# A shifted-window attention block and a ConvNeXt-V2 block in one launch: how the parameters and constants reach the chip

## What is computed

```
# block 0: window attention (7x7 windows, shifted by 3, 3 heads of 16), then an MLP
xw  = windows(roll(layernorm_over_channels(x) * norm1_g + norm1_b, -3, -3))      # 49 tokens each
q, k, v = split(xw @ qkv_w + qkv_b)
a   = softmax(q @ k.T * 16 ** -0.5 + bias)        # bias[h,i,j] = rel_bias_table[rel(i,j), h]
x   = x + roll(unwindow((a @ v) @ proj_w + proj_b), 3, 3)
x   = x + gelu(layernorm(x) @ fc1_w + fc1_b) @ fc2_w + fc2_b                     # 48 -> 192 -> 48
# block 1: depthwise 7x7 convolution, MLP with global response normalisation
y   = layernorm(dwconv7x7(x, dw_w) + dw_b) * ln_g + ln_b
y   = gelu(y @ w1.T + b1)
n   = sqrt(sum_over_pixels(y ** 2)); n = n / (mean_over_channels(n) + 1e-6)
x   = x + (grn_g * (y * n) + grn_b + y) @ w2.T + b2
```

## Time and profile before

| | us |
|---|---|
| median of 3 runs | 2145.37 |
| lowest and highest of the 3 | 2136.65, 2146.94 |
| profiled execution, whole | 2144.79 |
| profiled execution, span of the trace | 2142.8 |
| PE busy | 1776.0 (83%) |
| ACT busy | 1558.6 (73%) |
| DVE busy | 1510.8 (71%) |
| POOL busy | 1174.1 (55%) |
| hardware DMA queue, share of 16 engines | 43.0% |

### The profile page before, as it was taken

The page is one execution under the profiler, slowest core; times in us unless marked ns, Lnnn a source line. Parts: engine busy times, 40 slices in busy tenths (PEclk is TensorE's granted clock), DMA queues, the critical chain, the costliest instruction groups (busy, mean ns, idle before and its releaser), DMA issues. The chain is left out here.

```text
span 2142.8 us, 91033 instructions
## 1 busy us (share of the span) xinstructions
PE 1776.0 (83%) x38074; PEld 1038.0 (48%) x38074; DVE 1510.8 (71%) x2025; ACT 1558.6 (73%) x2884; POOL 1174.1 (55%) x1061
## 2 busy tenths in 40 slices
PE   1469889898989889898989898884799959888884
PEld 0245555555555555555555555551466622222221
DVE  1557878777787778777777878643677757767772
ACT  1458888888888888888888888873566648767770
POOL 1357777767677767777676777652255520111111
PEclk9979999999999999999999999995799967989998
DMA  2334343434434343434344353422378759988983
GB/s 21 76 92 114 88 117 85 114 96 103 103 96 110 89 119 84 115 90 108 98 102 104 96 114 87 100 50 63 85 217 217 214 121 189 225 213 209 229 206 106
DMA packets 241103, 260.66 MB, mean 122 GB/s; under 512 B 174431, under 2 KB 188148, under 8 KB 240713
## 3 DMA queue, kind: packets, MB, share of 16 engines
q1 hardware_dynamic: 225353, 215.94, 43.0%
q0 software_dynamic: 15360, 39.08, 6.3%
HBM read 159.26 MB, written 80.99 MB: 112 GB/s over the span
## 5 line engine op out<-in xcount | busy, mean ns | idle before, releaser
L439 POOL TENSOR_TENSOR shift<-const_b,qmax 113x588 bf16<-113x588 bf16 x256 | 344.6, 1347 | 53.9 <-DVE qmax L532 53.7
L464 POOL TENSOR_TENSOR xl<-x 113x784 bf16<-113x784 f32 x64 | 136.9, 2140 | 266.5 <-DVE x L554 266.5
L518 DVE TENSOR_TENSOR xh<-X,RS 113x784 f32<-113x784 f32 x64 | 228.7, 3573 | 19.2 <-DMA RS<-rs_scratch 18.4
L1505 POOL DMA_DIRECT2D out_rolled<-r_OUT x128 | 64.0, 503 | 322.3 <-DVE r_OUT L1607 319.3
L532 DVE TENSOR_REDUCE qmax<-ps_s 113x12 f32<-113x588 f32 x256 | 194.6, 760 | 61.4 <-PE ps_s L905 61.3
L758 ACT ACTIVATE G<-ps_m 128x392 f32<-128x392 f32 x384 | 184.1, 498 | 50.7 <-PE ps_m L1005 49.8
L726 ACT ACTIVATE P<-ps_t 113x588 f32<-113x588 f32 x256 | 171.9, 672 | 66.3 <-PE ps_t L955 65.5
L1340 PE MATMUL conv_ps<-xin,band_now 64*64 64x448 bf16 x2688 | 202.3, 364 | 4.1 <-DVE x_low L1242 4.1
L429 POOL TENSOR_TENSOR xhl<-xh 113x784 bf16<-113x784 f32 x64 | 203.4, 3178 | 2.5 <-DVE xh L572 2.5
L719 ACT COPY Uf<-ps_m 113x392 f32<-113x392 f32 x384 | 172.7, 485 | 32.1 <-PE ps_m L872 24.0
L524 DVE TENSOR_TENSOR Ul<-Uf 113x784 bf16<-113x784 f32 x192 | 180.6, 966 | 0.3 <-ACT Uf L719 0.2
(11 more groups left out here) (256 smaller groups left out, 5258.6 us busy)
## 6 DMA issues: line engine op xcount, KB each, us to landing
xin<-rows_scratch SPq DMA_DIRECT2D x96, 236.0 KB, 3.7
XT<-x_tokens SPq DMA_DIRECT2D x64, 294.0 KB, 4.7
X<-x_windows SPq DMA_DIRECT2D x128, 147.0 KB, 3.0
RS<-rs_scratch SPq DMA_DIRECT2D x128, 147.0 KB, 3.4
XR<-x_windows SPq DMA_DIRECT2D x128, 147.0 KB, 3.8
x_scratch<-x SPq DMA_DIRECT2D x128, 147.0 KB, 3.9
y_scratch<-y POOLq DMA_DIRECT2D x96, 196.0 KB, 2.8
r_RS<-rs_scratch SPq DMA_DIRECT2D x128, 147.0 KB, 3.9
```

The costliest lines, as they stand in the source:

```text
L439: nc.gpsimd.tensor_tensor(shift[:, j % 2], e, m, ALU.mult).then_inc(S["md"], 1)
L464: nc.gpsimd.tensor_tensor(xl1[:], x1[:, r, :], x1m[0][:, r, :], ALU.subtract).then_inc(S["x1_lo"], 1)
L518: nc.vector.tensor_tensor(xh0[:, r, :], X[:, r, :], RS[:, r, :], ALU.mult).then_inc(S["xh0"], 1)
```

## The change

All parameters and constants arrive in three arrays that the host lays out: `pack_a` (128 x 2039 f32) for the attention phase, `pack_c` (128 x 2176) for the convolution, `pack_r` (128 x 1160) for the last phase. Each is one tile, and the old names are views of it. The host also gathers the relative bias and casts the band constants.

```diff
-        center = sb("center", [R, R])
-        sums_f = sb("sums_f", [R, 2, R])
+        pack = sb("pack", [128, WIDE_A])
+        def packed(name, rows):
+            return pack[0:rows, PACK_A[name]]
+        center = packed("center", R)
+        sums_f = packed("sums", R).rearrange("p (a c) -> p a c", a=2)
...
-        CLEARS = 17
+        CLEARS = 5
-        SETUP_V = 41
-        BIAS_V = SETUP_V + 3
+        CLEAN_V, AUG_V, QK_V, GRAM_V, WV_V, SETUP_V = 5, 11, 13, 21, 25, 33
...
         def _(sp):
-            for tab, first, sign in ((tables[0], (REL - 1) * HEADS, -1), (tables[1], 0, 1)):
-                sp.dma_start(tab, bass.AP(tensor=prm["rel_bias_table"].tensor, offset=first,
-                                          ap=[[1, HEADS], [sign * HEADS, REL], [1, 1]]),
-                             allow_slow_non_contiguous=True).then_inc(table_turned, 16)
...
-            def later_loads():
-                sp.wait_ge(later["cleared"], len(later["zeros"]))
-                for dst, src in later["loads"]:
-                    sp.dma_start(dst, src).then_inc(later["loaded"], 16)
-                for row in edges:
+            def later_load(k):
+                dst, src = later["loads"][k]
+                sp.dma_start(dst, src).then_inc(later["loaded"], 16)
+            def margin_rows(k):
+                for row in edges[4 * k:4 * k + 4]:
                     sp.dma_start(rows_dram[:, row], margin[:].rearrange("c (b w) -> c b w", w=PAD)
                                  ).then_inc(margins_stored, 16)
...
-            sp.wait_ge(x_cleared, 6)
-            for raw in range(2):
-                tokens_load(Strip(0, raw, N))
-            setup_loads()
-            for raw in range(2 - TLEAD, -1):
-                step(Strip(0, raw, N), 0)
-            late_loads()
-            step(Strip(0, -1, N), 0)
-            later_loads()
-            for raw in range(N + 3):
+            tokens_load(Strip(0, 0, N))
+            sp.dma_start(pack[:], pack_a).then_inc(loaded, 16)
+            tokens_load(Strip(0, 1, N))
+            step(Strip(0, 2 - TLEAD, N), 0)
+            sp.wait_ge(x_cleared, 6)
+            for raw in range(3 - TLEAD, N + 3):
                 step(Strip(0, raw, N), (raw - 3) // STRIPS)
+                if raw in (STRIPS, STRIPS + 1):
+                    later_load(raw - STRIPS)
+                elif raw in (STRIPS + 2, STRIPS + 3):
+                    if raw == STRIPS + 2:
+                        sp.wait_ge(cleared, CLEARS)
+                    margin_rows(raw - STRIPS - 2)
...
         def _(pool):
-            for t in (proj_w, proj_b, fc2_b, w2_own, w2_part, bias_f, wv, wv_swap, *gram, *w1_own, *w1_part, margin, blank, x2):
+            for t in (wv, wv_swap, blank, margin, x2):
                 nc.gpsimd.memset(t[:], 0.0).then_inc(cleared, 1)
...
-            for raw in range(-4, -2):
+            for raw in range(-4, -1):
                 step(Strip(0, raw, N))
-            for t in later["zeros"]:
-                nc.gpsimd.memset(t, 0.0).then_inc(later["cleared"], 1)
-            steps(step, -2, N + 3)
+            for r in range(2):
+                pool.wait_ge(values_spread, 4 * r + 4)
+                nc.gpsimd.tensor_tensor(Ul[:, r, HEADS:, :], Uf[:, r, HEADS:, :], U[0][:, r, HEADS:, :], ALU.subtract
+                                        ).then_inc(values_low, 1)
+            steps(step, -1, N + 3)
...
 +            clear_inputs((X, RS), 0)
+            for t in (ps_t, ps_s, *ps_m):
+                link(nc.vector.memset(t[:], 0.0))
+            step(Strip(0, -4, N))
+            clear_inputs((XR,), 0)
+            clear_inputs((X, RS, XR), 1)
+            dve.wait_ge(loaded, 16)
...
 -                nc.scalar.preload_act_table_set("gelu_and_others")
+                if old.real:
+                    nc.scalar.preload_act_table_set("gelu_and_others")
...
-                nc.scalar.preload_act_table_set("natural_log_exp_and_others")
+                if old.real:
+                    nc.scalar.preload_act_table_set("natural_log_exp_and_others")
...
-            steps(step, -3, N + 2)
+            for raw in range(-3, -1):
+                step(Strip(0, raw, N))
+            act.wait_ge(setup_v, WV_V)
+            for r in range(2):
+                for a in range(2):
+                    for n, t in enumerate((wv, wv_swap)):
+                        nc.scalar.copy(
+                            Uf[:, r, HEADS + a, cols_of(n)].rearrange("p (w t) -> p w t", t=TOK),
+                            t[:, TOK * a:TOK * a + TOK].unsqueeze(1).to_broadcast([R, WINS // 2, TOK])
+                        ).then_inc(values_spread, 1)
+            steps(step, -1, N + 2)
...
 -            pe.wait_ge(setup_v, 6)
+            pe.wait_ge(setup_v, AUG_V)
...
-            pe.wait_ge(setup_v, SETUP_V)
+            pe.wait_ge(setup_v, GRAM_V)
...
+                    if s.n == 0 and j == 0:
+                        wait(pe, values_low, 2)
```

More of the change, by code:

```diff
@@ L244, in attention_phase @@
         x2_strips = x2_dram.rearrange("b c (g s i w) -> b s g c i w", g=2, s=STRIPS, i=WS)
[L247 to L270, removed]
-        blocks = []
-        for side in range(2):
-            for h in range(HEADS):
-                src = bass.AP(tensor=table_runs[side].tensor, offset=h * TOK * RUN,
-                              ap=[[RUN, TOK], [SPAN, WS], [1, WS]])
-                dst = bias_f[0:TOK, side, TOK * h:TOK * h + TOK]
-                blocks.append((dst.rearrange("p (a b) -> p a b", a=WS), src))
         block = ctx.enter_context(nc.Block())
@@ L608, in step, with clear_inputs @@
                 query_max(nxt, 1)
-            for t in (X, RS, XR):
-                for r in range(2):
+            def clear_inputs(tiles, r):
+                for t in tiles:
                     nc.vector.memset(t[:, r, :], 1.0).then_inc(x_cleared, 1)
-            for raw in range(-4, -2):
-                step(Strip(0, raw, N))
-            dve.wait_ge(cleared, CLEARS)
-            dve.wait_ge(loaded, 16 * len(loads))
+            clear_inputs((X, RS), 0)
+            for t in (ps_t, ps_s, *ps_m):
+                link(nc.vector.memset(t[:], 0.0))
+            assert chain[0] == CLEAN_V
+            step(Strip(0, -4, N))
+            clear_inputs((XR,), 0)
+            clear_inputs((X, RS, XR), 1)
+            dve.wait_ge(loaded, 16)
             link(nc.vector.tensor_copy(sum_w[:], sums_f[:]))
@@ L621, in _ @@
                 link(nc.vector.tensor_copy(aug[:, a, C:C + 1], norms[:, 2 * a + 1:2 * a + 2]))
+            assert chain[0] == AUG_V
+            step(Strip(0, -3, N))
             dve.wait_ge(setup_t, 1)
@@ L632, in _ @@
             link(nc.vector.tensor_tensor(out_b[:], proj_b[:], fc2_b[:], ALU.add))
-            splits = []
+            for g in range(2):
+                lo = ROWB * g
+                split(gram, lambda t: t[lo:lo + C + 1, :, lo:lo + C + 1],
+                      ps_s[lo:lo + C + 1, 0, 0:HEADS * (C + 1)].rearrange("p (h c) -> p h c", h=HEADS))
+            assert chain[0] == GRAM_V
+            dve.wait_ge(cleared, CLEARS)
             for g in range(2):
@@ L1826, in program @@
+def program(nc, x_in, x_tokens, packs, out_dram, images):
     scratch = {}
@@ L1837, in sb @@
             return ctx.enter_context(nc.sbuf_tensor(name, shape, dt))
-        tiles, zeros, loads = response_weights(nc, sb, layer1, con)
-        later = {name: ctx.enter_context(nc.semaphore("later_" + name)) for name in ("cleared", "loaded")}
+        tiles, loads = response_weights(nc, sb, packs[2])
+        later = {name: ctx.enter_context(nc.semaphore("later_" + name)) for name in ("loaded",)}
         with ExitStack() as inner:
@@ L1872 @@
     x_in, x_tokens = give("x_windows", windows), give("x_tokens", tokens_first(windows))
[L1873 to L1877 removed]
+    layers = [{k[8:]: np.asarray(a) for k, a in inputs.items() if k.startswith(f"L{n}_conv_")} for n in range(2)]
+    packs = [give("parameters_" + name, a) for name, a in zip("acr", packs_of(*layers, constants()))]
     out = nc.dram_tensor("out_rolled", (images, C, PLANE), F32, kind="ExternalOutput").ap()
[L1879 removed]
+    program(nc, x_in, x_tokens, packs, out, images)
     result = run_bass_kernel_spmd(nc, [arrays], core_ids=[0]).results[0]["out_rolled"]
```

247 lines of the change are left out of this document (127 added, 120 removed).

## The result

| | before | changed |
|---|---|---|
| median, us | 2143.34 (4 runs beside it) | 2075.66 (4 runs) |
| lowest and highest | 2136.65, 2146.94 | 2074.42, 2077.34 |
| ratio, 95% interval | | 0.9688 [0.9662, 0.9715] |
| profiled execution, and its span | 2144.79, 2142.8 | 2077.34, 2075.7 |

The changed kernel is 67.7 us faster by the medians and 67.1 by the spans; 2079 was forecast. Five more runs of it on another occasion gave 2073.53.

What follows compares the result with a forecast made beforehand. The attention pipeline's fixed beat was taken as unchanged, its start held back by setup and a stall. Setup 46.1 plus stall 19.6 gave 65.7 us off 2144.79, so 2079; range 2068 to 2096.

Steps and rivals of the forecast that it cites:

- Setup, 46.1: Before strip 0: first scores at 34.8 instead of 82.45, 47.6 us gained, less 1.5 for POOL's subtractions.
- This ends last, not the products: Setup: the root of strip 0 through DRAM, with xh done at 22.9, ends after the second products at 21.1.
- The collision, 1.5: Setup: POOL's two value subtractions overlap DVE's low halves and lengthen each other; nothing to 6 us, taken as 1.5.
- The stall, 19.6: Waits for strip 2's loads behind later loads and margin stores on SP's queue vanish: 16.6, 1.7 and 1.3 us gained.
- Below, 15.4: Lower bound of the stall's gain in us, PE's own idle time; the upper bound was 22.
- The clock's term, +1.7: Part of the stall's gain: without idle time PE's higher clock comes earlier, saving 1.7 us on 3.5 busy us.
- The tables: ACT's table loads go from steps 0 and 1: 1.28 us showing in step 0, 1.3 in step 1.
- Strips 8 to 11, nothing: Later packs and margin rows moved there fit into SP's 8.9 us wait per strip, so they cost nothing.
- 1: Rival: the stall returns in another form as DVE or PE meets another late piece; total 2096, chance 0.12.
- 2: Rival: the pack loads slowly at 86 GB/s and shifts the whole setup chain; total 2091, chance 0.09.
- 3: Rival: something that stays holds the start, so the gain is a third, 22 us; total 2123, chance 0.03.
- 4: Rival: slower, each of 62 strips starting at PE's lower clock, 1.7 us a time; total 2184, chance 0.02.

Runs made afterwards that it cites:

- packs_old_order: Changed kernel, three arrays and later loads at strips 8 to 11 kept, but DVE, ACT and POOL setup in the order of before: median 2092.11 us.
- values_low_dve: Changed kernel with the two low-half subtractions of the values back on DVE instead of POOL: 2079.13 us, a single run.
- before_later_moved: Kernel of before with only its 28 later loads moved behind steps 8 and 9 and its margin stores behind 10 and 11: median 2126.96 us.
- tables_always: Changed kernel with ACT's two table loads back in every step, also where no gelu follows: median 2074.28 us.
- later_first: Changed kernel with both later packs and all eight margin stores ahead of step 0 again: median 2073.2 us.
- both_again: Changed kernel with four later fills moved from DVE to POOL and the second buffer's values spread after step -1, rerun: median 2067.76 us.

## Why the prediction was right, and where its steps were not

- **The bound.** Right: what counted was when the beat begins. The beat stayed, and of the 66.05 us gained at strip 4, 65.1 stood at the first x_low of the convolution. That the total came so near is in part luck: against the forecast the setup gave 1.8 more, the stall 1.4 less, strips 8 to 11 took 1.0, and the later phases gave 2.0 that no step had.
- **Setup, 46.1.** 47.9 measured, 1.8 more. The pack was taken at 10.5, between 8.9 and 18; it landed at 6.8, so the low bound was the near one and still high. Its 2.3 us of fixed time follow from no row; a line through the two sizes of the earlier trace rows leaves 1.3. DVE free at 10.5 (10.6), first products at 14.8 (14.85) and second at 21.1 (21.17) were right to 0.1.
- **"This ends last, not the products"** failed. The way of the root was sized from the earlier trace rows, 3.3 us from the store's issue to that of RS; it took 1.6 (13.77 to 15.38). With the root 0.9 earlier too, xh began at 19.75, not 21.9, and the products with `gram` ended last: PE began at 23.63 instead of 24.5.
- **ACT's copies** to 28.6: they ended at 27.8, and first scores came 1.4 before the forecast.
- **The collision, 1.5.** Shown: the three low halves took 5.77 on DVE (three by 0.98 without POOL beside), and the first qmax followed the scores by 2.07 in place of 0.89, so 1.2. The Trainium skill (GPSIMD Engine Reference, section 4.1), which calls GpSimd about twice as slow for elementwise work with two inputs, is near: the same 1568 elements took 1.79 on DVE in packs_old_order and 2.78 on POOL, 1.55 times. It was not the slower engine but the lengthened DVE that cost the time, and values_low_dve shows that the cost equals the saving (35.51 against 35.48).
- **The stall, 19.6.** 18.2 measured (66.05 less 47.9). The term that was mis-sized is the first, 16.6: PE's idle time of 15.36 us did not turn into gain in full, and though the whole stall stayed above "Below, 15.4", the loads' part alone did not (13.1 in before_later_moved). The clock's term, +1.7, came to 2.3 by the count above (6.9 less 4.6), though not because "continuous work should bring the higher level earlier": the granted clock fell in the filling all the same, at 50 to 58 and 70 to 74. That leaves 15.9 where the forecast had 17.9 (16.6 and 1.3), about the shortfall of before_later_moved. Such a count is an estimate, since not all of that work is on the path. The tables were right, 2.72 for 2.6. The Trainium skill (ScalarE: Activation LUTs, What ACT_TABLE_LOAD costs) has 2.66 us per switch of set, which would be 5.3, an estimate, if one switch shows in each of the two steps; the run has half of it.
- **Strips 8 to 11, nothing.** About 1.0 us was lost: xh in the changed kernel came at 235.92, 257.56, 278.82, 299.89 and 320.89, so beats of 21.64, 21.26, 21.07 and 21.00. In PE's timeline one place shows it:

```profile
238.79 0.20 PE L956 MATMUL ps_o<-P,V 113*32 113x49 f32 x1 [0.70 <-issue]
```

  pack_r had gone out at 232.43 and took 4.5 us. That it is the cause is not shown: tables_always has the same load and keeps 21.00, and later_first, with no load there, has a beat of 21.37 at 300, which the next makes good (20.63). But the beat of strip 11 takes 21.38 to 21.92 in six of the ten traces that load pack_r there (21.00 to 21.12 in the other four), and 21.00 in both that load it earlier. PE waited for nothing the profile names.
- **The later phases, as long as before.** From the first x_low to the end: 618.9 before, 616.9 changed, 608.4 to 617.3 in the variants read, with the same instructions. Some 2 us of the 67.1 come from there and belong to no step. This is also why medians tell differences of 2 to 3 us badly. Marks in the attention phase tell them better (the two traces of the change differ by 0.3 at the first qmax and by 0.1 near 1203), though each mark is of one execution, and a stretched beat can shift it.
- **Rivals.** 1 fell: no wait of DVE over 3 us up to strip 3; the longest is 2.6, for rden. 2 and 3 fell with the pack at 6.8 and the first scores at 33.41. 4 fell for this kernel (1.00 in its steady windows), but single falls of this kind exist in three variants: in both_again behind strip 5 (two beats, 2.7 us too long together), in packs_old_order behind strip 15 (two beats, 4.4 too long) and in values_low_dve at 780 (one beat, 2.1 too long). In each of them the clock was back at 1.00 and the beat at 21 soon after, so none fed itself.

## What to carry to other kernels

When the start of a pipeline waits for parameters, count issues on the queue first: here one load of 1 MB landed in 5.5 us, where 28 small ones, behind an element-wise load and the tokens, ended at 45.93. Look at the length of each issue too: four of the 28 took two thirds of the time, and whether their number or the element-wise load ahead of them was to blame is not shown. Then order each engine's setup so that the first strip's work comes between the constants; that was a third of the setup's gain (16.1 of 47.9), and it needs no faster engine. Follow a gain at marks along the trace: an edit can lead by 1.4 us at the first strip and by nothing at the fourth.

## What the runs showed of the hardware

- While the pack of 1019.5 KB and the token loads beside it were under way, the DMA engines moved 301 to 489 GB/s in 13 of the 16 quarter microseconds from 2.5 to 6.5, well over the 254 of the earlier trace rows, a window of the steady state; the estimate from the small loads (86 GB/s) was far off.
- The same kind of load can take far longer behind an element-wise one: 294 KB of tokens landed in 15.7 us behind the turn of the bias table (507 single elements, twice), in 3.2 without it. From 6 to 12 us the DMA engines of the kernel before were busy 0.68 of the time and moved 5 GB/s.
- The granted clock falls towards its lower level (0.50, 1.2 GHz) while the pipeline fills, at other strips in each variant (50 to 58 in the changed kernel, 98 to 110 in before_later_moved), three times in the steady state (130 in both_again, 358 in packs_old_order, 780 in values_low_dve), and in later_first not at all from 30 to 110. What those windows cost is not shown: later_first has none of them and makes good 2.1 of its 2.7 us between strips 2 and 4, where the count for the changed kernel gives 4.6.
- POOL's four fills of 784 elements took 0.74 each beside DVE's memsets, against 0.71 on DVE, and DVE's own beside them kept their length (0.91 and 0.48): memsets do not lengthen each other here as the subtractions do. Small DVE instructions can suffer too: `aug<-pack` of 48 by 48 took 1.30 us beside POOL's centring in both_again, against 0.23 in the changed kernel.
